# The scan's three loop passes written out as straight code on four engines

## The chip, the cores and the metric

One Trainium2 chip, one core of it. The metric is the device time of one execution of the whole program in microseconds (us), and the median over the runs counts.

## The reference

The program computes four layers on `x` (16 sequences of 256 positions and 256 features), each conditioned on a vector per sequence. Layer 1 is a bidirectional selective state-space model, and its recurrence is the part that matters here. For each direction, sequence, inner channel d (512) and state s (64), it steps through the positions t:

```
dA  = exp(dt[t, d] * A[d, s])
h   = h * dA + (dt[t, d] * x[t, d]) * B[t, s]
y[t, d] = sum over s of h[d, s] * C[t, s]
```

Layers 0 (low-rank adapters), 2 and 3 (attention with an MLP) stand before and after it.

## The kernel before

`program` calls four functions, one after the other, with a barrier of all engines between them: `conditioning`, `prepare` (layer 0 and the projections, their results written to DRAM), `scan` (the recurrence) and `finish` (the rest of layer 1, then layers 2 and 3). Only `scan` is touched.

`scan` works in 4 sweeps (`SWEEPS`), one per direction and half of the channels. A sweep has 256 rounds, one per position, cut into 16 bodies of 16 rounds (`BODY`, `BODIES`). There are 64 bodies in all (`ALL`), numbered G = 0 to 63, and 1024 rounds, numbered n. The state of one round is four chunks k of 128 partitions by 512 elements.

In a round, PE makes the exponents of a later round (`adt`, L1249, into banks of `s_pa`), adds the product of B and dt*x to chunks 0 and 1 in `s_pA` or makes it for chunks 2 and 3 in `s_pB` (`bu`, L1259), and multiplies the state by C (`y`, L1286, into `s_py`). ScalarE takes the exponential (`take`, L1374, into `s_dec`) and copies chunks 0 and 1 out to `s_hs` (`copy_a`, L1380). VectorE multiplies chunks 0 and 1 by their decay in place (`times`, L1473) and adds chunks 2 and 3 (`plus`, L1484, into `s_hs`). GpSimd multiplies chunks 2 and 3 by their decay (`decayed`, L1444). There are two buffers of decays, each good for 8 rounds; rounds 0 and 8 of a body turn from one to the other (`dec_ready`). Once per body VectorE copies `s_py` out (`take_y`, L1490), PE transposes it (`turn_y`, L1298) and ScalarE copies it to `s_ys` (L1394).

Each engine has its own list of instructions in this order, written by hand; semaphores that only count up tie them together. Nearly every instruction is preceded by a wait for a count that follows from n, G or the number of the DMA (helper `wait`, L75 to L79). The engines' lists come from a function `body(G, made, first, last, head, turn)` each, called by `bodies` (L1119 to L1128). `made` is the number of GpSimd products before the body; `head` marks body 0, `first` a body that starts a sweep, `last` body 63, and `turn` is the count by which the A matrices of the next sweep have landed, for the last body of a sweep.

In the kernel before, body 0 is straight code, bodies 1 to 48 are a loop (`Fori`, L1123) of three passes with 16 bodies each, and bodies 49 to 63 are straight code again. Inside the loop the number of the pass is a register, so every count that depends on it is one, too. SP, which issues the DMAs of the scan, has straight code for all 64 bodies already. Loops of the same sort stand in `prepare` (L418) and in `finish` (L1586 and, for layers 2 and 3, L1943).

Of the kernel before, what the change touches and what calls it, by code (L numbers as in the profile page):

```python
# [1064 lines left out]
def scan(nc, ctx, io, keep, scratch):  # L1065

    SWEEPS = 4
# [17 lines left out]
    with ExitStack() as c:  # L1085
# [30 lines left out]
                             "y_mm", "filled", "taken", "c_filled", "ytok_done", "exp_ready"))  # L1116
        DQ, UQ, BQ = 16 * 4, 16 * CH, 16 * CH

        def bodies(eng, body):  # L1119

            made = 2 * T - 2
            body(0, 0, True, False, True, None)
            with eng.Fori(0, SWEEPS - 1) as i:  # L1123
                for q in range(1, BODIES + 1):
                    body(BODIES * i + q, made * i + 2 * (BODY * q - q // BODIES), q == BODIES, False, False,
                         64 * i + 128 if q == BODIES - 1 else None)
            for q in range(1, BODIES):
                body(ALL - BODIES + q, made * (SWEEPS - 1) + 2 * BODY * q, False, q == BODIES - 1, False, None)  # L1128

        def pair(G, x, w, head):  # L1130

# [22 lines left out]
        with nc.Block() as block:  # L1154
# [83 lines left out]
            def _(pe):  # L1238
# [121 lines left out]
                for k in range(2, CH):  # L1360
                    for v in range(2):
                        to_b(0, 0, 0, k, v)
                bodies(pe, body)
                y(BODY * ALL - 1, BODY - 1, 0)
                y(BODY * ALL - 1, BODY - 1, 1)
                p = 15 + 33 * (ALL - 1) + 17
# [2 lines left out]
            @block.scalar  # L1369
            def _(act):  # L1370
                def take(p, at, i, bank, w):

                    q, d = 2 * (at % 2) + i, 8 * (at // 2)
                    act.activation(  # L1374
                        dec[w][:].rearrange("p k i t d -> p (k i t) d")[:, :, DS * q + d:DS * q + d + 8],
                        pa[:, bank, :].rearrange("p (d c) -> p c d", d=8), ACT.Exp).then_inc(taken, 1)

                def copy_a(n, x, k):
                    wait(act, bu_a, 2 * n + k + 1)
                    act.copy(hs[k][:, x % 2, :], pA[:, k, :]).then_inc(copied, 1)  # L1380

                def take_pair(G, x, w, head):
                    p = pair(G, x, w, head)
                    wait(act, filled, p + 1)
                    for e in range(2):
                        take(p, 2 * (x % TB) + w, e, slot_bank(0, w, x, head, e), 1 - x // TB)

                def turned_y(p, G, banks):

                    wait(act, filled, p + 1)  # L1390
                    wait(act, y_out, 32 * (G - 1))
                    for v in range(2):
                        for h in range(2):
                            op = act.copy(ys[:, h].rearrange("p (k v) b t -> p v k b t", v=2)[:, v],  # L1394
                                          pa[:, banks[v], P * h:P * (h + 1)].rearrange(
                                              "p (k t b) -> p k b t", k=CH, b=PAIR))
                        op.then_inc(taken, 1)

                def body(G, made, first, last, head, turn):
                    for x in range(BODY):  # L1400
                        n = BODY * G + x
                        more = not (last and x >= TB)
                        copy_a(n, x, 0)
                        if more:
                            if x % TB == 0:
                                wait(act, mul, 2 * n)
                                wait(act, added, 2 * n)
                            take_pair(G, x, 0, head)
                        copy_a(n, x, 1)
                        if more:  # L1410
                            take_pair(G, x, 1, head)
                        if x == 2 and not head:
                            turned_y(15 + 33 * G + 6, G, [(12 + e) % BANKS for e in range(2)])

                act.activation(ys[:, 0, 0, 0, 0:1], keep["eps"][:], ACT.Exp).then_inc(exp_ready, 1)
                act.wait_ge(exp_ready, 1)
                for p in range(PAIRS):
                    act.wait_ge(filled, p + 1)
                    for e in range(2):
                        take(p, p, e, (2 * p + e) % BANKS, 0)  # L1420
                bodies(act, body)
                p = 15 + 33 * (ALL - 1) + 17
                turned_y(p, ALL, [(2 * p + e) % BANKS for e in range(2)])

            @block.gpsimd
            def _(pool):
                pool.memset(cz[:], 0.0).then_inc(zeroed, 1)
                pool.memset(one[:], 1.0).then_inc(zeroed, 1)
                pool.memset(ident[:], 0.0).then_inc(zeroed, 1)
                pool.wait_ge(zeroed, 3)  # L1430
                pool.affine_select(out=ident[:], in_=ident[:], compare_op=ALU.not_equal, fill=1.0, base=0,
                                   pattern=[[-1, P]], channel_multiplier=1).then_inc(const, 2)

                def fill(of):
                    lo = cz[:, :, 0:288].rearrange("p u (t w) -> p u t w", w=36)
                    hi = cz[:, :, 32:CW].rearrange("p u (t w) -> p u t w", w=34)
                    pool.tensor_tensor((hi if of else lo)[:, :, :, 0:PAIR], cl[:, :, 8 * of:8 * of + 8, :],
                                       one[:, None, None, 0:1].to_broadcast([P, UNITS, 8, PAIR]), ALU.mult
                                       ).then_inc(c_filled, 1)

                def decayed(n, x, k):
                    wait(pool, added, 2 * n - 3 + k)
                    m = of_chunk(k, x)
                    pool.tensor_tensor(m, two(hs[k][:, (x + 1) % 2, :]), m, ALU.mult).then_inc(m_done, 1)  # L1444

                def body(G, made, first, last, head, turn):
                    for x in range(BODY):
                        n = BODY * G + x
                        dec_ready(pool, G, x, head)
                        if not (first and x == 0):  # L1450
                            decayed(n, x, 2)
                            decayed(n, x, 3)
                        if x == 2:
                            wait(pool, y_mm, 32 * G)
                            fill(1)
                        if x == 10 and not last:
                            wait(pool, y_mm, 32 * G + 18)
                            wait(pool, c_in, 16 * (G + 2))
                            fill(0)

                pool.wait_ge(c_in, 16)
                fill(0)
                bodies(pool, body)

            @block.vector
            def _(dve):
                def times(n, x, k, first):
                    wait(dve, copied, 2 * n + k - 1)
                    if first:
                        dve.memset(pA[:, k, :], 0.0).then_inc(mul, 1)  # L1470
                    else:
                        state = two(pA[:, k, :])
                        dve.tensor_tensor(state, state, of_chunk(k, x), ALU.mult).then_inc(mul, 1)  # L1473

                def plus(n, made, x, k, first):
                    wait(dve, bu_b, 2 * n + k - 1)
                    if k == 2:
                        wait(dve, y_mm, 2 * n - 2)
                    out = two(hs[k][:, x % 2, :])
                    if first:  # L1480
                        dve.tensor_copy(out, two(pB[:, k - 2, :])).then_inc(added, 1)
                    else:
                        wait(dve, m_done, made + 2 * x + k - 3)
                        dve.tensor_tensor(out, two(pB[:, k - 2, :]), of_chunk(k, x), ALU.add).then_inc(added, 1)  # L1484

                def take_y(G):

                    wait(dve, y_mm, 32 * G)
                    wait(dve, filled, 33 * G - 11)
                    dve.tensor_copy(ytok, py[:]).then_inc(ytok_done, 1)  # L1490

                def body(G, made, first, last, head, turn):
                    for x in range(BODY):
                        n = BODY * G + x
                        start = first and x == 0
                        dec_ready(dve, G, x, head)
                        for k in range(2):
                            times(n, x, k, start)
                        if x == 1 and not head:
                            take_y(G)  # L1500
                        for k in range(2, CH):
                            plus(n, made, x, k, start)

                bodies(dve, body)
                take_y(ALL)
    release(nc, sems)

# [1070 lines left out]
```

## Time and profile before

| | us |
|---|---|
| median of 3 runs | 7390.89 (7389.54 to 7392.94) |
| the profiled execution, its own time | 7387.62 |
| its span, first to last instruction | 7385.8 |
| PE matmul busy in the span | 6787.5 (92%) |
| ScalarE busy | 4687.8 (63%) |
| VectorE busy | 4254.5 (58%) |
| GpSimd busy | 3328.7 (45%) |

The span is what the profile covers of one execution; 1.8 us of the execution's time lie around it. Matmuls are pipelined and their ends are modelled, so 92% doesn't say that PE works at its peak. The granted clock of PE is given as a share of the full 2.4 GHz: 0.50 is the lower of its two levels, 1.2 GHz. In the rows below, PE is the matmul side of TensorE, PEld the side that loads weights, and a q behind an engine's name (PEldq, DVEq) marks what its sequencer does by itself: register operations, branches, waits that are instructions of their own. A row of the timeline merges equal instructions that follow each other; in square brackets stands how long the engine was idle before, and what ended that.

### The profile page before, as it was taken

The numbers are of one execution on the slowest core, as the hardware profiler recorded it, in microseconds if no ns is written. First come the engines' busy times: TensorE is split into PE (matmuls) and PEld (weight loads), VectorE is DVE, ScalarE is ACT, GpSimd is POOL, SyncE is SP. The second block draws the span as 40 slices with busy tenths as digits, with TensorE's granted clock in tenths as the row PEclk, the third lists the DMA queues.
The fourth block names the chain that finished last, engine by engine and source line by source line (L and its number), as shares of the span: only waits on it lengthen the run. The fifth ranks groups of instructions, "written<-read, shape, count | busy, mean of one in ns | idle before, by whom it ended". The sixth has DMA issues, their size and how long they took to land. (4 is left out here: it accounts for less than half of the span.)

```text
span 7385.8 us, 182682 instructions
## 1 busy us (share of the span) xinstructions
PE 6787.5 (92%) x68920; PEld 3195.0 (43%) x68920; DVE 4254.5 (58%) x6974; ACT 4687.8 (63%) x9618; POOL 3328.7 (45%) x2814
## 2 busy tenths in 40 slices
PE   6888599999999999999999999997989999979888
PEld 3444344444444444444444444443444544535444
DVE  2555466666666666666666666664443543545554
ACT  3555477777777777778777788772234534435554
POOL 0101166666666666666666666661022322323333
PEclk8999755555555555555555555557999999989999
DMA  5555512121212212211122112215410000000000
GB/s 185 157 145 146 142 53 54 53 56 54 61 53 56 55 54 59 56 54 54 54 56 62 54 55 55 55 50 193 143 46 6 10 9 6 7 33 10 13 12 6
DMA packets 596322, 458.63 MB, mean 62 GB/s; under 512 B 449728, under 2 KB 504640, under 8 KB 577280
## 3 DMA queue, kind: packets, MB, share of 16 engines
q1 hardware_dynamic: 594624, 445.32, 20.8%
q8 instruction: 567, 9.29, 0.5%
q14 instruction: 299, 2.45, 0.1%
q10 hardware_dynamic: 832, 1.57, 0.1%
HBM read 301.29 MB, written 145.49 MB: 60 GB/s over the span
## 5 line engine op out<-in xcount | busy, mean ns | idle before, releaser
L1444 POOL TENSOR_TENSOR s_dec<-s_hs,s_dec 128x512 f32<-128x512 f32 x2040 | 2553.2, 1276 | 1467.0 <-DVE s_hs L1484 890.8
L1374 ACT ACTIVATE s_dec<-s_pa 128x512 f32<-128x512 f32 x4096 | 2236.7, 602 | 95.2 <-PE s_pa L1249 38.7
L1286 PE MATMUL s_py<-s_hs,s_cz 128*32 128x256 f32 x16384 | 2183.6, 630 | 0.0
L1473 DVE TENSOR_TENSOR s_pA<-s_pA,s_dec 128x512 f32<-128x512 f32 x2040 | 1397.5, 696 | 965.0 <-ACT s_hs L1380 639.8
L1380 ACT COPY s_hs<-s_pA 128x512 f32<-128x512 f32 x2048 | 1218.7, 595 | 711.5 <-PE s_pA L1259 710.7
L1249 PE MATMUL s_pa<-s_dl,s_al 18*128 18x64 bf16 x32768 | 1545.8, 235 | 88.6 <-DMA s_dl<-D 48.6
L1484 DVE TENSOR_TENSOR s_hs<-s_pB,s_dec 128x512 f32<-128x512 f32 x2040 | 1324.8, 686 | 401.6 <-PE s_py L1286 311.9
L1259 PE MATMUL s_pA<-az 18*128 18x256 bf16 x4096 | 1194.1, 399 | 77.4 <-DVE s_pA L1473 71.4
L1249 PEld LDWEIGHTS s_pa<-s_dl,s_al 18*128 18x128 bf16 x32768 | 1172.8, 120 | 182.6 <-issue 57.6
L1259 PE MATMUL s_pB<-az 18*128 18x256 bf16 x4096 | 1225.6, 399 | 19.9 <-DVE s_hs L1484 19.9
L1259 PEld LDWEIGHTS s_pB<-az 18*128 18x128 bf16 x4096 | 261.9, 102 | 1583.5 <-issue 862.8
L2039 POOL TENSOR_TENSOR t_prob<-t_prob,t_rinv 128x512 f32<-128x512 f32 x512 | 529.3, 1041 | 508.0 <-DVE t_rinv L2412 507.9
L2277 ACT ACTIVATE t_prob<-t_ps,t_nmax 128x256 f32<-128x256 f32 x1024 | 480.1, 483 | 275.2 <-DVE t_nmax L2418 274.3
L1286 PEld LDWEIGHTS s_py<-s_hs,s_cz 128*32 128x32 f32 x16384 | 422.6, 141 | 441.3 <-issue 356.7
L2418 DVE TENSOR_REDUCE t_nmax<-t_ps 128x2 f32<-128x512 f32 x512 | 347.2, 681 | 174.6 <-PE t_ps L2099 172.5
L1259 PEld LDWEIGHTS s_pA<-az 18*128 18x128 bf16 x4096 | 320.5, 101 | 214.3 <-issue 105.9
L2114 PE MATMUL t_ps<-t_ident,t_prob 128*128 128x128 f32 x2048 | 281.9, 280 | 43.1 <-ACT t_probt L2284 24.5
L2078 PE MATMUL t_ps<-t_h,t_wqkv 128*128 128x512 f32 x640 | 294.7, 606 | 11.9 <-DVE t_h L2338 11.9
L2099 PE MATMUL t_ps<-t_k,t_q 64*128 64x256 f32 x2048 | 292.2, 407 | 9.0 <-ACT t_prob L2277 9.0
L2114 PEld LDWEIGHTS t_ps<-t_ident,t_prob 128*128 128x128 f32 x2048 | 221.4, 142 | 137.9 <-issue 75.0
L2060 PE MATMUL t_ps<-t_h,t_w 128*128 128x512 f32 x512 | 243.9, 632 | 30.2 <-DVE t_h L2338 26.8
L547 POOL TENSOR_TENSOR p_ur<-p_u,p_up 128x2048 f32<-128x2048 f32 x16 | 65.1, 4071 | 402.2 <-ACT p_up L827 402.2
(254 smaller groups left out, 5966.6 us busy)
## 6 DMA issues: line engine op xcount, KB each, us to landing
s_dl<-D SPq DMA_DIRECT2D x512, 144.0 KB
az<-U SPq DMA_DIRECT2D x1024, 72.0 KB
az<-B SPq DMA_DIRECT2D x1024, 36.0 KB
D<-p_dp SPq DMA_DIRECT2D x64, 384.0 KB, 5.8
U<-p_up SPq DMA_DIRECT2D x60, 384.0 KB, 6.1
B<-p_bz SPq DMA_DIRECT2D x144, 128.0 KB, 2.5
SZ<-p_sz SPq DMA_DIRECT2D x16, 1024.0 KB, 4.0
SK<-p_skip SPq DMA_DIRECT2D x16, 1024.0 KB, 5.8
```

Source lines behind the costliest of these rows:

```text
L1249: mm = pe.matmul(pa[:, banks[e], DS * i:DS * (i + 1)], al[QR * q:QR * q + ROWS, d, :], dl[w[0]][QR * q:QR * q + ROWS, :, d, :], start=True ...
L1259: mm = pe.matmul(out[:, HALF * v:HALF * (v + 1)], bl[j % 2][r, t, v, :], ul[j % 2][r, v, t, :], start=first, stop=True, skip_group_check=n ...
L1286: mm = pe.matmul(py[QR * k:QR * (k + 1), HALF * v:HALF * (v + 1)], cz[:, 2 * k + v, at:at + QR], hs[k][:, x % 2, HALF * v:HALF * (v + 1)], ...
L1374: act.activation(dec[w][:].rearrange("p k i t d -> p (k i t) d")[:, :, DS * q + d:DS * q + d + 8], pa[:, bank, :].rearrange("p (d c) -> p ...
L1380: act.copy(hs[k][:, x % 2, :], pA[:, k, :]).then_inc(copied, 1)
L1444: pool.tensor_tensor(m, two(hs[k][:, (x + 1) % 2, :]), m, ALU.mult).then_inc(m_done, 1)
L1473: dve.tensor_tensor(state, state, of_chunk(k, x), ALU.mult).then_inc(mul, 1)
L1484: dve.tensor_tensor(out, two(pB[:, k - 2, :]), of_chunk(k, x), ALU.add).then_inc(added, 1)
L2039: pool.tensor_tensor(prob[at][:], prob[at][:], rinv[at][:, :, None].to_broadcast([P, 2, T]), ALU.mult).then_inc(s["norm"], 1)
L2114: mm = pe.transpose(ps[:, SR + n % 2, kb * T + e * P:kb * T + (e + 1) * P], prob[n % RING][:, e, kb * P:(kb + 1) * P], ident[:])
L2277: op = act.activation(prob[at][:, b, :], ps[:, n % SR, b * T:(b + 1) * T], ACT.Exp, bias=nmax[at][:, b:b + 1], accum_out=rsum[at][:, b:b + 1])
L2418: dve.tensor_reduce(nmax[n % RING][:], ps[:, n % SR, :].rearrange("p (a t) -> p a t", t=T), axis=AX.X, op=ALU.max, negate=True).then_inc(s ...
```

## The change

`bodies` no longer makes a loop. It calls `body` 64 times with whole numbers, on PE, ScalarE, GpSimd and VectorE alike. The arguments have the same values as the loop's expressions gave in each pass. SP's code, the operations, their order and their tiles are the same.

```diff
-        def bodies(eng, body):
-
-            made = 2 * T - 2
-            body(0, 0, True, False, True, None)
-            with eng.Fori(0, SWEEPS - 1) as i:
-                for q in range(1, BODIES + 1):
-                    body(BODIES * i + q, made * i + 2 * (BODY * q - q // BODIES), q == BODIES, False, False,
-                         64 * i + 128 if q == BODIES - 1 else None)
-            for q in range(1, BODIES):
-                body(ALL - BODIES + q, made * (SWEEPS - 1) + 2 * BODY * q, False, q == BODIES - 1, False, None)
+        def bodies(body):
+
+            for G in range(ALL):
+                sweep, g = G // BODIES, G % BODIES
+                turn = g == BODIES - 1 and G < ALL - 1
+                body(G, 2 * (BODY * G - sweep), g == 0, G == ALL - 1, G == 0, 64 * (sweep + 2) if turn else None)
...
-                bodies(pe, body)
+                bodies(body)
...
-                bodies(act, body)
+                bodies(body)
...
-                bodies(pool, body)
+                bodies(body)
...
-                bodies(dve, body)
+                bodies(body)
```

## Rows read from the trace of the kernel before

**Rows 1.** The page: span, busy time of each engine, the larger instruction queue.

```profile
span 7385.8 us, 182682 instructions
...
PE 6787.5 (92%) x68920; PEld 3195.0 (43%) x68920; DVE 4254.5 (58%) x6974; ACT 4687.8 (63%) x9618; POOL 3328.7 (45%) x2814
...
q8 instruction: 567, 9.29, 0.5%
```

**Rows 2.** Busy time by stretch: us from A to B, then length and engines.

```profile
2215.41:2279.78 64.37, 62.60 (x907) 27.05 (x900) 42.23 (x65) 50.80 (x100) 40.80 (x35) 0.50 0.20 54
4204.81:4268.87 64.06, 62.43 (x903) 26.90 (x902) 42.52 (x65) 50.81 (x100) 40.78 (x35) 0.50 0.20 55
995.28:4076.69 3081.41, 2982.40 (x43208) 1289.17 (x43202) 2025.27 (x3121) 2437.29 (x4800) 1951.79 (x1627) 0.51 0.20 56
4076.69:4966.85 890.16, 865.51 (x12603) 373.03 (x12602) 594.45 (x911) 710.52 (x1400) 570.97 (x477) 0.51 0.20 55
4585.64:4646.55 60.91, 58.35 (x903) 25.11 (x902) 42.04 (x66) 50.33 (x100) 40.78 (x35) 0.58 0.21 58
```

**Rows 3.** Timeline of VectorE, L1484 in rounds 0 and 1: bodies 21 and 52.

```profile
2279.78 0.69 DVE L1484 TENSOR_TENSOR s_hs<-s_pB,s_dec 128x512 f32<-128x512 f32 x1
...
2283.75 0.68 DVE L1484 TENSOR_TENSOR s_hs<-s_pB,s_dec 128x512 f32<-128x512 f32 x1
...
4268.87 0.69 DVE L1484 TENSOR_TENSOR s_hs<-s_pB,s_dec 128x512 f32<-128x512 f32 x1
...
4272.62 1.28 DVE L1484 TENSOR_TENSOR s_hs<-s_pB,s_dec 128x512 f32<-128x512 f32 x2
```

**Rows 4.** Instructions of the wait helper, L79: loop body 19, straight body 50.

```profile
L79 DVEq ALU_OP  x82: 40/40/45, 2151.1 to 2214.3; - x82
L79 PEldq FUSED_REGOPS  x54: 42/46/60, 2151.1 to 2214.8; - x54
...
L79 PEldq EVENT_SEMAPHORE  x24: 51/51/51, 4145.8 to 4204.7; - x24
```

**Rows 5.** Timeline of VectorE, first L1484 of rounds 8 and 9: bodies 0, 20, 51.

```profile
964.32 0.69 DVE L1484 TENSOR_TENSOR s_hs<-s_pB,s_dec 128x512 f32<-128x512 f32 x1
...
967.53 1.29 DVE L1484 TENSOR_TENSOR s_hs<-s_pB,s_dec 128x512 f32<-128x512 f32 x2
...
2248.73 0.69 DVE L1484 TENSOR_TENSOR s_hs<-s_pB,s_dec 128x512 f32<-128x512 f32 x1
...
2252.08 1.29 DVE L1484 TENSOR_TENSOR s_hs<-s_pB,s_dec 128x512 f32<-128x512 f32 x2 [0.22 <-PE s_py L1286]
...
4237.92 0.69 DVE L1484 TENSOR_TENSOR s_hs<-s_pB,s_dec 128x512 f32<-128x512 f32 x1
...
4241.13 1.29 DVE L1484 TENSOR_TENSOR s_hs<-s_pB,s_dec 128x512 f32<-128x512 f32 x2
```

**Rows 6.** PE's branches: nanoseconds least/median/most of the scan's loop, then of the later ones.

```profile
L1123 PEldq COMPARE_BRANCH  x3: 82/3617/4411, 2017.3 to 4073.6; - x3
L1943 PEldq COMPARE_BRANCH  x4: 83/1784/3742, 5847.6 to 7068.9; - x4
L1586 PEldq COMPARE_BRANCH  x2: 83/158/234, 5190.9 to 5263.7; - x2
```

**Rows 7.** Timeline where the second pass begins: weight loads of PE, then VectorE.

```profile
2021.98 0.10 PEld L1259 LDWEIGHTS s_pA<-az 18*128 18x128 bf16 x1 [3.26 <-issue]
...
2025.28 0.13 PEld L1249 LDWEIGHTS s_pa<-s_dl,s_al 18*128 18x128 bf16 x3 [3.06 <-issue]
...
2020.35 0.69 DVE L1484 TENSOR_TENSOR s_hs<-s_pB,s_dec 128x512 f32<-128x512 f32 x1
...
2029.44 0.68 DVE L1484 TENSOR_TENSOR s_hs<-s_pB,s_dec 128x512 f32<-128x512 f32 x1
```

**Rows 8.** VectorE where the third pass begins.

```profile
3049.58 0.69 DVE L1484 TENSOR_TENSOR s_hs<-s_pB,s_dec 128x512 f32<-128x512 f32 x1
...
3057.60 1.27 DVE L1484 TENSOR_TENSOR s_hs<-s_pB,s_dec 128x512 f32<-128x512 f32 x2
```

## The prediction

> **What bounds the kernel now.** I read the page first: PE is busy for 6787.5 of 7385.8 us, far ahead of the other engines [rows 1]. Then I cut the scan into bodies, each from the first L1484 write of its round 0 to that of the next, and asked for the busy time by stretch. A plain body takes 64.37 us in the loop and 64.06 us in the straight code behind it; PE is busy for 62.60 and 62.43 of them, ScalarE for 51, and PE's granted clock is 0.50, its level of 1.2 GHz [rows 2]. So PE's work carries the scan, and what the change can give lies in the 1.8 us of a body in which PE has no matmul, and at the edges between passes.
>
> The trace of before holds the kernel after in small: bodies 0 and 49 to 63 are already straight code with whole numbers in the waits. Bodies 1 to 48 are the loop. The prediction is mostly a comparison of the two.
>
> **Part 1: the register work before the waits.** In a loop body the wait helper issues 82 ALU_OP on VectorE at 40 ns (3.3 us) and 54 FUSED_REGOPS on PE at 46 ns (2.5 us), with others of the kind; in a straight body PE has only 24 EVENT_SEMAPHORE left [rows 4]. Most of it lies beside other work: the sequencers run ahead of their engines. It shows only where all engines wait for each other in turn, in the rounds where the decay buffers change. From the first L1484 of round 0 to that of round 1 are 2283.75 - 2279.78 = 3.97 us in the loop and 4272.62 - 4268.87 = 3.75 us in straight code [rows 3]. From round 8 to round 9 are 3.35 us in the loop and 3.21 us in straight code; body 0, which is straight code at the other end of the scan, has 967.53 - 964.32 = 3.21 us as well [rows 5]. That speaks for the form of the code and against the place in the scan as the cause. These two are 0.22 + 0.14 = 0.36 us; the whole body differs by 64.37 - 64.06 = 0.31 us, so the rest gives 0.05 us back. I take 0.31. Over the 48 loop bodies that is 48 x 0.31 = 14.9 us. From both sides: nothing, if all of it belonged to the place, and 48 x 0.36 = 17.3 us.
>
> **Part 2: the edges between passes.** The loop's branch is executed three times, and PE's takes 4411, 3617 and 82 ns; the last is the one that leaves the loop [rows 6]. Behind the first, PE's weight loads stand still twice, for 3.26 us and 3.06 us, with nothing but issue before them. Round 0 of body 17 then lasts 2029.44 - 2020.35 = 9.09 us, against the plain 3.97: 5.12 us too long [rows 3, 7]. At the next edge it is 3057.60 - 3049.58 = 8.02 us, 4.05 us too long [rows 8]. Straight code has no branch there, so both go: 9.17 us. ScalarE, VectorE and GpSimd lose their branches too, but at these edges they wait for PE's products anyway, and what the four stalls cost together is in the two rounds. Nothing else is late in their place, since the rounds behind the exit of the loop run at the plain 3.75. Between zero (if the stall only moves) and 2 x (3.26 + 3.06) = 12.6 us I take 9.2, as the rounds measure it.
>
> The Trainium skill has two rules on this. "Runtime: NRT & Kernel Launch", section on instruction fetch mechanics, says that fetching runs ahead in straight order only and that a taken branch out of the fetched window has to wait for its target. The PE rows of the branch agree: 3.6 to 4.4 us where it is taken, 0.08 us where it is not. "Advanced Engine Details and Errata", section on control flow timing, gives about 108 ns for a compare and branch; by it the two edges would be worth an estimated 0.2 us, and the kernel would come out at about 7370.5 us instead of the time below. The row of the untaken branch fits that figure, the taken ones don't.
>
> **Part 3: what the clock gives.** PE is mostly granted 1.2 GHz here, but some bodies have a short stretch at 2.4 GHz and are shorter: the body at 4585.64 took 60.91 us at a mean clock of 0.58 [rows 2]. What they are worth in all is worked out from sums. Bodies 49 to 62: 14 x 64.06 = 896.8, measured 890.16, so 6.7 us in 14 bodies, 0.48 us each. Bodies 1 to 48: 48 x 64.37 + 9.2 = 3099.0, measured 3081.41, so 17.6 us, 0.37 us each [rows 2]. After the change all bodies are of the straight kind, and I take the straight rate: 48 x 0.48 = 23.0 us instead of 17.6, 5.4 us more. It is the weakest term: 14 bodies are few, and a body of another length meets these stretches elsewhere. Its ends are a rate of zero (17.6 us lost) and the whole difference of the body at 4585.64, 3.15 us, in every second body (76 us instead of 17.6, 58 us gained).
>
> **Part 4: what else moves.** The edges with a change of sweep (bodies 15, 31, 47 and the ones behind them) have their waits for the A matrices in PE as constants; the loads stay with SP, whose code was straight before. No data transfer moves by more than the 0.3 us of a body. The code of `finish` lies elsewhere in memory now. PE's branch there takes 3.74 us at most in L1943 and at most 0.23 us in L1586 [rows 6]; which of these prices a loop pays may change with its place. L1586 could pay 3.5 us more, and the two taken branches of L1943 (one in layer 2, one in layer 3) 3.5 us less each. I put it at 0, between +3.5 and -7.
>
> **The sum.** 14.9 + 9.2 + 5.4 = 29.5 us less. The profiled execution, at 7387.62 us (1.8 us around its span), would come to 7358.1. It lies 3.3 us under the median of the runs, so from 7390.89 the forecast is 7361.4 us. The change that a measurement can tell from none is 0.2%, or 15 us; the forecast is twice that.
>
> **The rivals.**
> *The edges are paid back by the clock.* At the first edge PE's long stall is followed by a stretch at 2.4 GHz. If the stalls brought such stretches about and straight code has none to spare, part 2 is worth only what the edges cost net, and part 3 falls to the rate of zero at worst: 14.9 + 9.2 - 17.6 = 6.5 us less, 7384.4 us, within 0.2%. Against it: the straight bodies 49 to 62 have 6.7 us of such gifts with no stall before them.
> *Many more stretches at 2.4 GHz.* Straight bodies that are 0.31 us shorter may meet them more often. At twice the straight rate (0.95 us a body) the sum falls by a further 23 us: 7338 us. The body at 4585.64 shows that one can be worth 3.15 us; that only 14 bodies in straight code have been seen speaks neither way.
> *Straight code starves PE of instructions.* Slower. The place is PE's sequencer in bodies 1 to 48, which now runs through new addresses instead of ones it has seen. If it caught up with its fetching once per body, each time would cost a stall like the 3.06 us behind the branch [rows 7]: 48 x 3.06 = 147 us, so 7361.4 + 147 = 7508 us. It decides from 29.5 / 3.06, some 10 such stalls, on. Against it: bodies 49 to 63 run on in just this way without one, and the instruction queue moved 9.29 MB for PE's 2 x 68920 matmuls and weight loads, 67 bytes for each that was executed; so the loop saved no fetching before, each pass was fetched anew [rows 1].
> *The waits cost nothing and the place does.* If the 0.31 us of a body came from the last sweep's place, part 1 is gone: 7361.4 + 14.9 = 7376.3, at the border of no change. Body 0's 3.21 us in round 8 speak against it.
>
> **How the numbers follow.** Forecast (part 1 and 2 in full, the clock's share anywhere between 0.2 and 0.8 us a body): 0.76. Many more stretches: 0.08. Edges paid back: 0.06. The place: 0.05. Starved: 0.05. The first two are faster by over 0.2%, so is half of the place's case: 0.87. Within 0.2% are the paid-back case and the rest of the place's: 0.09. Slower: 0.04, since a few stalls only would leave the starved case at no change. The forecast's own range is 7346 (0.8 us a body) to 7378 (0.2 us a body and 3.5 us for L1586). With part of the neighbouring cases I give 7341 to 7379.
>
> **What would show it.** Right, if loop line L1123 is gone from all engines, the helper's register operations on PE and VectorE are zero in the scan, plain bodies take 64.06 us from 1 to 62, round 0 of bodies 17 and 33 takes 3.75 us, and the instruction queue moves a little less than 9.29 MB. Wrong in part 1, if plain bodies of the first three sweeps stay at 64.37. Wrong in part 2, if issue stalls of about 3 us stand anywhere in PE's straight code. Wrong in part 3, if 63 bodies times 64.06 less the measured scan is far from 30 us. Of the rest, a difference of over 7 us outside the scan would mean that the moved code of the later stages matters more than I allow.

## The result and the profile after

The kernel after takes 7351.03 us, median of 5 runs (7348.0 to 7354.67), against 7390.89 us (5 runs, 7388.4 to 7392.94). The ratio is 0.9945, 95% interval 0.9931 to 0.996: 39.9 us less, where 29.5 us less were forecast. The profiled execution took 7348.0 us.

The page after, its span, busy times and PE's instruction queue, answers to [rows 1]:

```profile
span 7346.2 us, 171571 instructions
...
PE 6757.2 (92%) x68920; PEld 3178.1 (43%) x68920; DVE 4265.1 (58%) x6974; ACT 4683.9 (64%) x9618; POOL 3326.2 (45%) x2814
...
q8 instruction: 545, 8.93, 0.5%
```

The numbers of matmuls and of the other engines' operations are the same. On balance 11111 instructions are gone: 13075 register operations and 12 branches, against 1976 plain waits (EVENT_SEMAPHORE) that came for them. The median and the profiled execution differ by 3 us, so the sums below are those of one execution.

Busy time by stretch, kernel after (us from A to B, length, busy time and count of PE, PEld, DVE, ACT, POOL, granted clock, DMA share, GB/s). First bodies 1 to 48, then 49 to 62, then bodies 20, 21 and 17. They answer to [rows 2]:

```profile
996.68:4038.95 3042.27, 2955.15 (x43203) 1274.07 (x43202) 2035.79 (x3121) 2434.95 (x4800) 1949.89 (x1627) 0.52 0.21 56
4038.95:4924.75 885.80, 859.84 (x12603) 370.58 (x12602) 593.81 (x911) 709.98 (x1400) 570.89 (x477) 0.52 0.20 55
...
2202.24:2266.31 64.07, 62.43 (x903) 26.89 (x902) 42.53 (x66) 50.82 (x100) 40.82 (x35) 0.50 0.20 55
2266.31:2327.26 60.95, 58.37 (x903) 25.08 (x901) 42.09 (x66) 50.33 (x100) 40.77 (x35) 0.58 0.21 57
2013.57:2075.47 61.90, 59.62 (x903) 25.79 (x902) 42.29 (x65) 50.54 (x100) 40.78 (x35) 0.56 0.21 56
```

Where the 39.6 us between the two spans went, by these boundaries:

| stretch | before | after | difference |
|---|---|---|---|
| up to body 1 | 995.28 | 996.68 | +1.4 |
| bodies 1 to 48 | 3081.41 | 3042.27 | -39.1 |
| bodies 49 to 62 | 890.16 | 885.80 | -4.4 |
| body 63 and what follows | 2418.95 | 2421.45 | +2.5 |

Bodies 49 to 62 are straight code in both kernels, and yet they differ by 4.4 us. That is the first sign that something apart from the code has a share.

Timeline of VectorE in body 33, where the third pass began before; it answers to [rows 8] (a line of `scan` has moved up by 4, so L1480 is the old L1484):

```profile
3025.17 0.69 DVE L1480 TENSOR_TENSOR s_hs<-s_pB,s_dec 128x512 f32<-128x512 f32 x1
...
3028.93 1.28 DVE L1480 TENSOR_TENSOR s_hs<-s_pB,s_dec 128x512 f32<-128x512 f32 x2
```

Round 0 takes 3.76 us instead of 8.02. The wait helper in body 20 (engine, operation, count: ns least/median/most) has nothing left but waits, as in the straight part of [rows 4]:

```profile
L79 DVEq EVENT_SEMAPHORE  x35: 21/21/1806, 2203.4 to 2266.2; - x35
L79 PEldq EVENT_SEMAPHORE  x24: 51/51/51, 2207.3 to 2266.2; - x24
```

Of PE's branches behind the scan, compare [rows 6], L1939 is the old L1943 and L1582 the old L1586:

```profile
L1939 PEldq COMPARE_BRANCH  x4: 83/1982/4019, 5806.2 to 7027.6; - x4
L1582 PEldq COMPARE_BRANCH  x2: 76/146/217, 5151.4 to 5224.2; - x2
```

They nearly kept their prices (4.0 us at most instead of 3.7, and 0.2 us as before), so the moved code matters little.

The sum for bodies 1 to 48: plain bodies are 64.07 us, so 48 x 0.30 = 14.4 us; the two edges are 9.2 us; and the clock gave 48 x 64.07 - 3042.27 = 33.1 us instead of 17.6, that is 15.5 us more. 14.4 + 9.2 + 15.5 = 39.1 us.

### The profile page after: what moved, and what is told of

Its sections match the earlier page's. It is cut to its first block and busy times, and to the rows that moved or that the text cites. A ratio compares the mean times of both kernels' runs of the same rounds, so it can differ in the third digit from the quotient of the medians.

```text
span 7346.2 us, 171571 instructions
## 1 busy us (share of the span) xinstructions
PE 6757.2 (92%) x68920; PEld 3178.1 (43%) x68920; DVE 4265.1 (58%) x6974; ACT 4683.9 (64%) x9618; POOL 3326.2 (45%) x2814
## 3 DMA queue, kind: packets, MB, share of 16 engines
q8 instruction: 545, 8.93, 0.5%
## 5 line engine op out<-in xcount | busy, mean ns | idle before, releaser
L1480 DVE TENSOR_TENSOR s_hs<-s_pB,s_dec 128x512 f32<-128x512 f32 x2040 | 1325.2, 686 | 374.1 <-PE s_py L1282 280.2
L1255 PE MATMUL s_pA<-az 18*128 18x256 bf16 x4096 | 1178.2, 396 | 72.1 <-DVE s_pA L1469 68.9
L2095 PE MATMUL t_ps<-t_k,t_q 64*128 64x256 f32 x2048 | 291.7, 407 | 9.1 <-ACT t_prob L2273 9.1
L2056 PE MATMUL t_ps<-t_h,t_w 128*128 128x512 f32 x512 | 243.3, 631 | 29.4 <-DVE t_h L2334 26.8
```

Source lines behind the costliest of these rows:

```text
L1255: mm = pe.matmul(out[:, HALF * v:HALF * (v + 1)], bl[j % 2][r, t, v, :], ul[j % 2][r, v, t, :], start=first, stop=True, skip_group_check=n ...
L2056: mm = pe.matmul(ps[:, jobs.bank(name), :], w, v, start=(k == 0), stop=(k == len(pairs) - 1))
```

## The experiments

In those that keep a loop on some engines, `looped(eng, body)` is the `bodies` of the kernel before, and `bodies(body)` that of the kernel after. The counts are the same in both, so the engines can be mixed. Where no number of runs is given, there was one, and its profile carries the verdict.

**One engine's loop at a time: PE.**

```diff
-                bodies(body)
+                looped(pe, body)
```

> The loop of three passes on PE alone; ScalarE, VectorE and GpSimd run straight code. Theory: the stall at the edges between passes is PE's own branch, so round 0 of bodies 17 and 33 is again 4 to 5 us longer than 3.75 us, while plain bodies stay within 0.1 us of 64.07 us, since the register work that shows is VectorE's. Rival 1: the edge costs what the four branches cost together; then PE's alone gives clearly less than 4 us. Rival 2: PE's 54 FUSED_REGOPS per body carry the 0.31 us; then plain bodies take 64.3 us or more.

7373.26 us. Timeline of VectorE in body 17 of this kernel (L1491 is the old L1484), then PE's branch:

```profile
2015.72 0.69 DVE L1491 TENSOR_TENSOR s_hs<-s_pB,s_dec 128x512 f32<-128x512 f32 x1
...
2023.72 1.28 DVE L1491 TENSOR_TENSOR s_hs<-s_pB,s_dec 128x512 f32<-128x512 f32 x2
```

```profile
L1130 PEldq COMPARE_BRANCH  x3: 83/3751/3957, 2012.6 to 4055.4; - x3
```

Round 0 takes 8.00 us, 4.25 us more than plain (at body 33, by the same reading, 4.3 us), and plain bodies stay at 64.07 us. So the long stall at an edge is PE's, and PE's 54 FUSED_REGOPS per body cost nothing. The theory held on both points. Neither edge is followed by a stretch at 2.4 GHz: bodies 17 and 33 stay at 0.50.

**VectorE alone.** The same edit with `looped(dve, body)`.

> The loop on VectorE alone. Theory: VectorE's 82 ALU_OP per body carry most of part 1, so plain bodies of the first three sweeps take 64.25 to 64.37 us against 64.07 us in the last sweep, round 0 takes about 3.95 us, and the edges cost under 0.5 us. Rival: the 0.31 us is made of small parts of all four engines; then plain bodies stay under 64.15 us.

7372.01 us. Body 19, a plain one in the second pass, of the kernel with VectorE's loop, then its bodies 1 to 48:

```profile
2144.39:2208.69 64.30, 62.43 (x911) 26.90 (x904) 42.10 (x66) 50.81 (x100) 40.78 (x35) 0.50 0.19 54
996.37:4056.41 3060.04, 2963.47 (x43212) 1278.34 (x43206) 2017.96 (x3121) 2435.77 (x4800) 1951.20 (x1627) 0.51 0.20 56
```

A plain body takes 64.30 to 64.31 us: VectorE's register work carries 0.24 of the 0.30 us. Round 0 of bodies 17 and 33 is 4.07 us, as in its neighbours, so its branch costs nothing.

**ScalarE and GpSimd.** `looped(act, body)` and `looped(pool, body)`.

> The loop on ScalarE and GpSimd, straight code on PE and VectorE. With VectorE's loop alone plain bodies took 64.31 us, with PE's alone 64.07, with all but PE's 64.37. Theory: ScalarE and GpSimd give the missing 0.06 us only together with VectorE, and nothing by themselves: plain bodies 64.07 to 64.13 us. The 0.9 to 1.0 us that the edges cost with all but PE's loop is ScalarE's code fetched again after its branch: round 0 or 1 of bodies 17 and 33 is about 1 us longer than plain. Rival: that edge cost needs VectorE's branch (VectorE's alone gave 0.0 us), and then nothing shows here.

7373.46 us. Bodies 18 and 17 of that kernel, and ScalarE's timeline behind its branch (L1381 takes the exponents):

```profile
2080.69:2144.82 64.13, 62.42 (x901) 26.91 (x900) 42.47 (x65) 50.80 (x101) 40.83 (x35) 0.50 0.20 55
2014.56:2080.69 66.13, 62.60 (x901) 26.71 (x900) 42.72 (x66) 50.89 (x101) 40.80 (x35) 0.50 0.20 52
```

```profile
2016.83 0.61 ACT L1387 COPY s_hs<-s_pA 128x512 f32<-128x512 f32 x1
2019.18 1.08 ACT L1381 ACTIVATE s_dec<-s_pa 128x512 f32<-128x512 f32 x2 [1.74 <-issue]
```

Plain bodies are 0.06 us longer, the rest of part 1. Body 17 is 66.13 - 64.13 = 2.0 us longer: ScalarE stands for 1.74 us with nothing but issue before it, shortly behind its branch. Body 33 is 65.71 us long, 1.6 us more than plain. The edges cost more than the 1 us expected, most of it in round 1 (2024.23 - 2018.82 = 5.41 us by the same view, plain 4.01). The branch itself lasts 0.06 us, at 2012.0; the next record of ScalarE's sequencer stands at 2015.3, and the stall of 1.74 us comes a few instructions later. GpSimd had its loop as well here, and what its branch adds was not separated.

**All but PE.**

> PE in straight code, the loop on ScalarE, VectorE and GpSimd. Theory: plain bodies take 64.25 to 64.37 us as in the kernel before, but rounds 0 of bodies 17 and 33 are not longer than 4.3 us, because the edge was PE's. As plain bodies are as long as before, the time that the clock gives back falls to about 0.37 us a body, and the kernel takes 7375 to 7385 us. Rival: the clock's share belongs to PE's straight code and stays at 0.68 us a body; then the kernel takes about 7366 us.

7392.0 us, longer than both predictions. Bodies 20 and 17, and bodies 1 to 48:

```profile
2158.18:2222.55 64.37, 62.42 (x907) 26.92 (x900) 42.24 (x65) 50.81 (x100) 40.79 (x35) 0.50 0.20 54
2026.83:2093.80 66.97, 62.60 (x907) 26.72 (x900) 42.53 (x65) 50.80 (x100) 40.81 (x35) 0.50 0.20 53
1000.91:4082.23 3081.32, 2979.37 (x43208) 1284.53 (x43202) 2026.27 (x3121) 2438.01 (x4800) 1952.08 (x1627) 0.51 0.20 56
```

ScalarE behind the same edge:

```profile
2032.28 1.08 ACT L1381 ACTIVATE s_dec<-s_pa 128x512 f32<-128x512 f32 x2 [2.09 <-issue]
```

Plain bodies are as long as in the kernel before, and an edge costs 2.6 us even without PE's branch. ScalarE's stall is there again, 2.09 us long. When all engines have their loops it hardly shows: the two edges cost 9.2 us then, and 8.6 us with PE's loop alone. "Not longer than 4.3 us" for round 0 was wrong (4.85 us at 17, 4.94 at 33). What the clock gave in this one execution is 48 x 64.37 + 2 x 2.6 - 3081.32 = 13.6 us, 0.28 us a body, with PE in straight code throughout. So PE's straight code alone doesn't bring the large share of the kernel after.

**What the clock gives, against the length of a body.** The kernel after with one memset more in round 0:

```diff
                         dec_ready(dve, G, x, head)
+                        if x == 0:
+                            dve.memset(idle[:], 0.0)
```

> The kernel after with one more VectorE memset (128x256 f32, to a tile that nothing reads) ahead of the first multiply of each body's round 0. Theory: what the clock gives depends on the length of the body and not on the form of the code. The memset makes plain bodies about 0.3 us longer (64.3 to 64.4 us), the clock's share falls from 0.68 to about 0.37 us a body as in the loop before, and the kernel takes 7351 + 64 x 0.3 + 64 x 0.3 = about 7390 us, 7380 at least. Rival: the share belongs to straight code; it stays at 0.68 us a body and the kernel takes 7351 + 19 = 7370 us.

10 runs: median 7371.35 us, but from 7351.37 to 7384.03, where the kernel before stayed between 7381.89 and 7394.68. In the profile a plain body is 64.31 us; bodies 1 to 48 and 49 to 62 read

```profile
997.52:4058.67 3061.15, 2964.26 (x43210) 1278.23 (x43204) 2040.34 (x3170) 2436.01 (x4800) 1950.30 (x1627) 0.51 0.20 56
4058.67:4954.94 896.27, 869.09 (x12610) 374.84 (x12604) 595.91 (x926) 711.10 (x1400) 570.96 (x477) 0.51 0.20 54
```

so the clock gave 48 x 64.31 - 3061.15 = 25.7 us (0.54 a body), then 4.1 us (0.29). Both predictions missed: neither 7390 nor a constant 0.68. VectorE's loop makes bodies of the same length in another way, and there the clock gave 48 x 64.31 - 3060.04 = 26.8 us (0.56 a body), nearly as much. The median alone would have supported the rival by accident; the spread of 33 us speaks against any steady share.

**The kernel after once more**, without an edit:

> The kernel after, unchanged, to see how much its time and the clock's share vary from execution to execution. Theory: bodies of 64.07 us meet the stretches at 2.4 GHz in a pattern that repeats, so the time stays within 4 us of 7351 us. Rival: the share is as loose as in the kernel with the memset (7351 to 7384 us), and the 7351 us of the first five runs were luck.

5 runs: median 7351.12 us, 7345.61 to 7360.61; ratio to the kernel before 0.9943 (0.993 to 0.9957). The profiled run was the slowest of them, 7360.61 us. Bodies 1 to 48:

```profile
998.79:4046.97 3048.18, 2962.49 (x43203) 1277.49 (x43202) 2036.17 (x3120) 2435.59 (x4800) 1948.82 (x1627) 0.51 0.20 56
```

Its share is 48 x 64.07 - 3048.18 = 27.2 us instead of 33.1, with bodies of the very same length. "Within 4 us" was too narrow; the median held.

**A longer memset.** To the memset of 128x256 one of 128x512 f32 was added in the same place:

```diff
+                            dve.memset(idle[:], 0.0)
+                            dve.memset(ytok, 0.0)
```

> The kernel after with two more VectorE memsets (128x256 and 128x512 f32) ahead of the first multiply of each body's round 0, which make plain bodies about 0.7 us longer (64.8 us). Theory: what the clock gives hangs on the length of the body, through which bodies end up where a stretch at 2.4 GHz can start; from the gains and places seen in the traces so far I work out a share that falls to 0.2 to 0.3 us a body at this length. The kernel then takes 7351 + 45 + 25 = about 7420 us. Rival: the clock's share stays at 0.5 to 0.7 us a body; then the kernel takes 7396 to 7408 us.

4 runs: median 7442.87 us, 7441.33 to 7443.02; ratio to before 1.0072 (1.0055 to 1.0089). Body 17, then bodies 1 to 48:

```profile
2037.60:2102.46 64.86, 62.44 (x910) 26.90 (x904) 43.16 (x69) 50.82 (x100) 40.85 (x35) 0.50 0.20 53
1000.03:4112.77 3112.74, 2996.49 (x43210) 1291.16 (x43204) 2070.51 (x3217) 2439.34 (x4800) 1954.20 (x1627) 0.50 0.20 55
```

48 x 64.86 = 3113.3: the clock gave nothing in 48 bodies; not one stretch at 2.4 GHz stands in them. Bodies 49 to 62 have none either. The work costs 64 x 0.79 = 51 us, the missing share the other 41 of the 91.8 us. A constant share (7396 to 7408 us) is ruled out. My own figure, 0.2 to 0.3 us a body (7420 us), was still too high.

**How long a pass may be.** On PE only, 14 passes of one body, then 7 of two:

```diff
+            with eng.Fori(0, BODIES - 2) as i:
+                body(i + 1, 0, False, False, False, None)
...
+            with eng.Fori(0, BODIES // 2 - 1) as i:
+                for q in range(2):
+                    body(2 * i + BODIES + 1 + q, 0, False, False, False, None)
```

> PE alone has loops: bodies 1 to 14 in 14 passes of one body (some 1930 PE instructions a pass), bodies 17 to 30 in 7 passes of two (some 3860). Everything else is straight. Theory: a taken branch stalls PE when its target has been dropped from the fetched code; of the loops so far, passes of some 370 and 500 PE instructions branched in 0.2 us, passes of 2200, 2600 and 30500 in 3.5 to 4.4 us. So each of the six edges between passes of two bodies costs about 4 us in its round 0 (7.9 to 8.1 us instead of 3.75), and the passes of one body cost nothing or, if 1930 is too many already, the same 4 us each. Rival: the stall belongs to the first round of a sweep (body 17) and not to the branch's distance; then neither kind of edge shows more than 0.3 us.

7426.59 us. PE's branches of the two loops, the weight loads behind the first edge (body 2), and the busy time of bodies 2 to 14, each of which begins behind a taken branch:

```profile
L1129 PEldq COMPARE_BRANCH  x14: 83/3556/3807, 1056.4 to 1943.0; - x14
L1133 PEldq COMPARE_BRANCH  x7: 83/3557/3840, 2196.0 to 2970.5; - x7
```

```profile
1059.94 0.10 PEld L1270 LDWEIGHTS s_pA<-az 18*128 18x128 bf16 x1 [2.14 <-DVE s_pA L1484]
...
1063.29 0.13 PEld L1260 LDWEIGHTS s_pa<-s_dl,s_al 18*128 18x128 bf16 x3 [3.11 <-issue]
```

```profile
1059.44:1946.10 886.66, 814.54 (x11719) 351.59 (x11720) 555.41 (x845) 660.58 (x1300) 530.16 (x443) 0.50 0.19 52
```

Both loops pay about 3.6 us per taken branch, so the stall has nothing to do with a sweep's beginning, and passes of one body (1911 PE instructions by the trace) are too long already. With passes of one body, round 0 took 7.24 to 8.45 us: 4.2 us too long on average, two stalls. With passes of two it took 5.96 to 6.63 us: about 2.5 us too long, and the second stall was missing at four of the six edges and 1.5 us long at the two others. So an edge costs one stall or two, which "4 us each" overlooked. What decides between them is open; the place of the code in memory was not varied by itself. In bodies 2 to 14 there is no stretch at 2.4 GHz at all, and of the six bodies behind the other edges two have one (19 and 21), so the stalls at edges are not what brings such stretches about.

**The other stages' loops.** First the one before the scan:

```diff
-            with eng.Fori(1, UNITS - 2) as i:
+            for i in range(1, UNITS - 2):
```

> The kernel after with the loops of the stage before the scan (L418) written out as well, those behind the scan left. Theory: the pass of that stage lasts 99.1 us in the loop and 95.6 us written out, as in the kernel without any loop; the scan starts about 17 us earlier and the kernel takes about 7334 us. Rival: part of the 17 us came with the other loops, and the gain is under 12 us, 7339 us or more.

4 runs: median 7333.87 us, 7330.47 to 7336.03; ratio to before 0.9923 (0.9907 to 0.994). Then all of them:

> The kernel after with the loops of the other stages written out as well, on all engines. Theory: PE's two taken branches of layers 2 and 3 (4.02 and 3.88 us) go, each with the second stall behind it; the four passes of the preparing stage save little, since PE's branch takes 0.2 us there. 8 to 14 us less than the kernel after: 7337 to 7343 us. Rival: in these stages the branch lies beside the softmax of ScalarE and VectorE and nothing shows: 7348 to 7353 us.

5 runs: median 7331.56 us, 7324.83 to 7336.22; ratio to before 0.9919 (0.9905 to 0.9932). It beats both kernels, by 62.3 us the one before and by 19.6 us the one after. In its profiled execution the scan starts 17.4 us earlier than in the kernel after (917.45 against 934.81 us), and body 63 with what follows takes 7.3 us less, close to the 8 us expected at least; 3.5 us of them are won before the first attention product of layer 2 (L2095). That part, kernel after, then all loops written out:

```profile
4924.75:7346.20 2421.45, 2196.91 (x9956) 1115.27 (x9954) 1161.12 (x2338) 1037.07 (x2875) 669.90 (x629) 0.95 0.11 38
```

```profile
4908.83:7323.00 2414.17, 2190.57 (x9956) 1112.66 (x9954) 1156.85 (x2338) 1036.59 (x2875) 669.41 (x629) 0.95 0.11 38
```

The medians of the last two kernels differ by 2.3 us only, less than the spread of either, so what the loops behind the scan are worth is read from the profiles alone. The surprise is the preparing stage, from which I had expected little. One pass of it in the kernel after, then in the kernel without loops:

```profile
365.43:464.45 99.02, 81.13 (x233) 46.10 (x233) 52.28 (x62) 52.46 (x50) 10.68 (x4) 0.93 0.54 146
```

```profile
359.70:455.26 95.56, 79.45 (x232) 46.00 (x233) 52.38 (x62) 52.46 (x50) 10.69 (x4) 0.95 0.56 152
```

ScalarE's timeline in that pass, kernel after, then the kernel without loops:

```profile
378.08 1.88 ACT L832 CAST p_up<-p_ur 128x2048 bf16<-128x2048 f32 x1
383.32 1.28 ACT L779 ACT_TABLE_LOAD   x1 [3.35 <-PE p_g L622]
384.61 1.88 ACT L779 ACTIVATE p_xs<-p_g 128x2048 f32<-128x2048 f32 x1
```

```profile
372.35 1.88 ACT L832 CAST p_up<-p_ur 128x2048 bf16<-128x2048 f32 x1
374.25 1.28 ACT L779 ACT_TABLE_LOAD   x1
377.11 1.88 ACT L779 ACTIVATE p_xs<-p_g 128x2048 f32<-128x2048 f32 x1 [1.57 <-PE p_g L622]
```

The activation of L779 reads PE's product `p_g`, and a table load stands directly ahead of it. In straight code the load follows the cast at once, and only the activation waits for PE. In the loop the count is a register, and the wait helper's register operations stand ahead of the table load. The first of them on ScalarE is

```profile
L79 ACTq ALU_OP  x2: 35/36/38, 383.1 to 383.2; - x2
```

and PE's product of L622 ends at 383.1 too. So the table load begins only when the product is there, and the activation comes 1.29 us behind it. The taken branch is not what delays the load. The first pass has none before it, and its load waits as well:

```profile
185.16 1.28 ACT L779 ACT_TABLE_LOAD   x1 [3.17 <-PE p_g L622]
```

Counted from the same VectorE operation (L918) in both passes, the activation is 1.58 us late in the loop. PE, which waits for what follows from it, then has been idle for 2.46 us instead of 0.95, and four matmuls of L649 then run at the lower clock, which makes another 1.7 us; the rest of the 3.46 us is spread over the pass. PE's clock there, kernel after, then without loops:

```profile
387.30:391.40 4.10, 4.01 (x8) 2.01 (x9) 2.60 (x5) 3.02 (x5) 0.00 (x0) 0.60 0.92 252
```

```profile
379.80:384.00 4.20, 4.11 (x12) 3.17 (x13) 2.73 (x5) 3.02 (x5) 0.00 (x0) 1.00 0.96 260
```

I had looked at PE's branch alone (0.2 us here) and expected nothing; 3.46 us a pass times 5 passes are the 17 us.

## Why the prediction came out as it did

*Part 1, register work (14.9 us).* Right: 14.4 us. That straight code and not the place in the scan makes the 0.3 us is shown: plain bodies are 64.07 us from 1 to 62. The engine is VectorE (0.24 us) with ScalarE and GpSimd (0.06 us), not PE.

*Part 2, the edges (9.2 us).* Right in size, since it was read from the rounds. PE's branch alone makes 4.3 us of each. The sentence that the other engines wait there anyway hid something: without PE's branch an edge still costs 1.6 to 2.0 us with loops on ScalarE and GpSimd, and 2.6 us with VectorE's too. Of the Trainium skill's two rules, the first one, that a taken branch out of the fetched window waits for its target ("Runtime: NRT & Kernel Launch", instruction fetch mechanics), is the one the runs bear out. (By the second rule the prediction's own terms add up to 7370.4, not 7370.5 us.) The same section of the Trainium skill gives PE room for 2048 instructions, the other engines for 512. The trace agrees only in part: PE's branch cost 0.2 us in passes of some 370 and 500 instructions and 3.3 us or more in those of 1911 and up, although 1911 is under 2048. As far as these loops show, the price sets in somewhere between 500 and 1911.

*Part 3, the clock (5.4 us).* The mis-sized term. The prediction took 0.48 us a body for straight code, from 14 bodies, and left bodies 49 to 62 alone. Measured were 33.1 us in bodies 1 to 48 (0.69 a body) and 11.2 us in 49 to 62 (0.80): 15.5 and 4.4 us more than before instead of 5.4 and 0. Together 14.5 us more than forecast, of which the other stages took 3.9 us back. The prediction had named its own sign for this: 63 bodies times 64.06 less the measured scan far from 30 us. Measured were 45.8 us, 2.2 of them because body 0 is short. It was right that this term was the weakest, and that "a body of another length meets these stretches elsewhere". It was wrong to carry a mean of 14 bodies to 62: the same straight bodies 49 to 62 got between 6.4 and 11.2 us in the traces of the kernels before, after and with loops on some engines. The second profile of the unchanged kernel after gave 27.2 and 7.7 us, so how far the term was off hangs on the execution as well, and that 7351 us lies within the stated range is in part luck.

*Part 4.* Right: later branches kept their prices, and at the turns of the sweeps nothing was lost (bodies 15 and 16 together took 63.71 + 64.31 us, no more than two plain ones).

*The rivals.* Paid back by the clock: wrong, it gave more, and 15 edges with PE's loop (2 with three passes, 13 with passes of one body) had no stretch at 2.4 GHz in the body behind them. Many more stretches: about half of it came in one execution, a fifth in the other. Starved straight code: PE's queue moved 8.93 MB, and the longest stall for issue of its weight loads between 997 and 4980 us is 1.0 us. The place: wrong.

What the term hangs on is open. Shares of the clock in bodies 1 to 48, one profiled execution each:

| plain body, us | kernel | us a body |
|---|---|---|
| 64.07 | after; after once more | 0.69; 0.57 |
| 64.07 | after, other loops written out (preparing stage; all) | 0.62; 0.66 |
| 64.07 | PE's loop: (48 x 64.07 + 8.6 - 3061.1) / 48 | 0.48 |
| 64.13 | loops of ScalarE and GpSimd | 0.44 |
| 64.31 | VectorE's loop; one memset | 0.56; 0.54 |
| 64.37 | before; all loops but PE's | 0.37; 0.28 |
| 64.86 | two memsets | 0 |

That the longest bodies get nothing is firm: four runs lie within 2 us of each other. Below that, the length alone doesn't order the shares, and with a spread of 33 us between executions of one kernel a single trace proves little. For the longest bodies the length isn't separated from the place of the added work either, since the memsets stand in round 0 alone. Shifting the start of the scan changed nothing that stands out. With the preparing stage written out, the same scan code starts 16.6 us earlier than in the kernel after, and its share lies between those of two executions of the kernel after:

```profile
980.11:4025.89 3045.78, 2959.82 (x43203) 1276.12 (x43202) 2036.53 (x3120) 2435.22 (x4800) 1949.95 (x1627) 0.51 0.20 56
```

## What to carry to other kernels

Where a kernel has the same code in a loop and written out, cut its trace at the same instruction of each repetition and compare plain ones; that priced the register work to 0.3 us in 64 and the edges to within the measured rounds. Look for the price of a loop behind the branch, on every engine, and not in the branch's own duration. Look too at what stands between a wait and the operation that needs it: a wait for a count in a register also held up the table load behind it, which in straight code went ahead. Before you call an instruction late, see whether it is late in a pass with no branch before it. A gain through the clock is no constant of the code: leave it a range from nothing to everything that one repetition has been seen to get, and don't read a median of such runs as proof of a mechanism.

## What the runs showed that I had not expected

More work can cost more than itself: 0.79 us of idle memsets per body cost 1.43 us per body (91.8 us in 64), because the granted clock then stayed at 0.50 throughout the scan. The same program spread over 33 us from run to run at one length (64.31 us), over 15 us at another (64.07 us) and over 2 us at a third (64.86 us).
